# Second cross-attention of a Perceiver block: rounding the scaled values on GpSimd and VectorE in f16, and a third probability copy for VectorE in every fourth head

## The reference, cut to what matters

```python
q = _fq_sym(q, axis=-1); k = _fq_sym(k, axis=-1)
v = _fq_sym(v, axis=2)                   # s = max|v| over the tokens / 127; round(v / s) * s
attn = softmax(einsum('bhqd,bhkd->bhqk', q, k))
attn = _fq_unsigned(attn, axis=-1)       # s = max / 255; round(attn / s) * s
out = einsum('bhqk,bhkd->bhqd', attn, v)
```

## Time and profile before

| | |
|---|---|
| median of 3 runs | 692.86 us (692.32 to 695.34) |
| the profiled execution | 691.79 us, span 689.9 us from the first to the last instruction |
| the stage of the change | about 360 to 570 us of the span |
| VectorE, ScalarE, TensorE, GpSimd busy from 458 to 470 us | 11.93, 11.93, 10.00, 11.02 of 12 us |
| mean granted TensorE clock | 0.921 of full speed |

### The profile page before, as it was taken

The page is one execution under the profiler, slowest core; times in us unless marked ns, Lnnn a source line. Parts: engine busy times, 40 slices in busy tenths (PEclk is TensorE's granted clock), DMA queues, the critical chain, the costliest instruction groups (busy, mean ns, idle before and its releaser), DMA issues. The chain is left out here.

```text
span 689.9 us, 12529 instructions
## 1 busy us (share of the span) xinstructions
PE 599.5 (87%) x4685; PEld 407.8 (59%) x4685; DVE 482.6 (70%) x793; ACT 383.2 (56%) x722; POOL 330.0 (48%) x264
## 2 busy tenths in 40 slices
PE   4976899997899999988876698888988877989997
PEld 3542445444677777676752455565555565668886
DVE  4357999995565664367686899999999956433322
ACT  4227975551432222155876799999999954321110
POOL 1009999995122332033432898989899840000000
PEclk9999999997999999999995678898878889999999
DMA  8526500000936555025563888988798738900000
GB/s 345 238 74 263 228 0 1 0 1 4 298 114 209 196 175 182 11 67 152 158 183 91 166 166 155 168 137 189 135 174 156 144 63 340 385 1 1 0 1 16
DMA packets 97090, 92.89 MB, mean 135 GB/s; under 512 B 70595, under 2 KB 88323, under 8 KB 93638
## 3 DMA queue, kind: packets, MB, share of 16 engines
q1 hardware_dynamic: 84352, 85.74, 45.7%
q10 hardware_dynamic: 12678, 6.36, 3.2%
HBM read 68.59 MB, written 6.62 MB: 109 GB/s over the span
## 5 line engine op out<-in xcount | busy, mean ns | idle before, releaser
L2074 DVE TENSOR_REDUCE d_nmax<-d_psum 128x1 f32<-128x1024 f32 x128 | 152.2, 1215 | 5.8 <-PE d_psum L2230 5.8
L2230 PE MATMUL d_psum<-kst,qT 96*128 96x512 bf16 x256 | 96.6, 477 | 31.8 <-ACT d_e L2171 12.9
L528 POOL TENSOR_TENSOR b_h<-b_h,b_cb 128x1024 f32<-128x1024 f32 x32 | 88.0, 2749 | 6.5 <-DVE b_h L578 6.0
L2054 POOL TENSOR_SCALAR d_rounded<-d_e,d_lift 128x1024 f16<-128x1024 f32 x64 | 73.2, 1144 | 13.4 <-issue 7.4
L2171 ACT ACTIVATE d_e<-d_psum,d_nmax 128x1024 f32<-128x1024 f32 x64 | 71.3, 1117 | 12.7 <-DVE d_nmax L2074 12.1
L2054 POOL TENSOR_SCALAR d_rounded<-spare,d_lift 128x1024 f16<-128x1024 f32 x62 | 70.1, 1131 | 14.4 <-ACT d_lift L2175 10.2
L578 DVE TENSOR_TENSOR_SCAN b_h<-b_dA,b_psum 128x1024 f32<-128x1024 f32 x32 | 73.2, 2286 | 2.5 <-ACT b_dA L633 2.0
L2171 ACT ACTIVATE spare<-d_psum,d_nmax 128x1024 f32<-128x1024 f32 x64 | 71.3, 1118 | 1.9 <-DVE d_nmax L2074 1.9
L633 ACT ACTIVATE b_dA<-b_dtT,b_A 128x248 f32<-128x248 f32 x128 | 53.7, 490 | 33.1 <-DVE b_h L578 28.1
L2257 PEld LDWEIGHTS d_psum<-d_ident_f,d_rounded 128*128 128x128 f16 x512 | 45.4, 123 | 32.1 <-issue 21.6
L689 PE MATMUL b_psum<-b_bdiag,b_dtx 128*128 128x512 f32 x128 | 60.2, 594 | 0.8 <-DVE b_h L578 0.8
(11 more groups left out here) (430 smaller groups left out, 1168.7 us busy)
## 6 DMA issues: line engine op xcount, KB each, us to landing
c_w<-in_w0gu SPq DMA_DIRECT2D x16, 768.0 KB, 4.8
kst<-kT_scratch SPq DMA_DIRECT2D x84, 128.0 KB, 2.7
w<-in_w SPq DMA_DIRECT2D x5, 1920.0 KB, 21.3
b_cb<-c_scratch SPq DMA_DIRECT2D x4, 2048.0 KB, 7.0
c_w<-in_w0dn SPq DMA_DIRECT2D x16, 384.0 KB, 5.5
kT_scratch<-k_kT ACTq DMA_DIRECT2D x15, 384.0 KB, 2.8
a_ctx<-in_ctx SPq DMA_DIRECT2D x2, 2048.0 KB, 19.8
k_ctxT<-in_ctxT SPq DMA_DIRECT2D x12, 256.0 KB, 3.1
```

The source lines that it names most:

```text
L528: nc.gpsimd.tensor_tensor(hv, hv, cv, ALU.mult).then_inc(hc_ready, 1)
L2054: nc.gpsimd.tensor_scalar(tile_of(r, j), e[j], lift[t][:, f:f + 1], HALF_ULP_ONE, ALU.mult, ALU.add).then_inc(r_ready, 1)
L2074: nc.vector.tensor_reduce(nm[:, t, m:m + 1, f:f + 1], quarter(m, j).unsqueeze(1), AX.X, ALU.max, negate=True).then_inc(nm_ready, 1)
L2230: last = nc.tensor.matmul(quarter(m, j)[:, b * 512:(b + 1) * 512], qT[0:QROWS, m:m + 1, t * P:(t + 1) * P], kst[m % 2][0:QROWS, at:at + 51 ...
```

## The change

The values are now rounded in two steps. GpSimd takes the scaled values, multiplies by a column of ones and adds 1536 into an f16 tile (`lift_values`); VectorE subtracts 1536 from that tile. `lift_values(m)` is issued in GpSimd's pass m when j is 5, that is between the roundings of units 4 and 5, and VectorE's `round_values(m)`, still at the end of its pass, now waits for it. Besides, in passes where (m - 1) mod 4 is 3, the turned unit 7 is copied by VectorE and not by ScalarE.

```diff
+HALFWAY = 1536.0
...
-    EVEN = tuple(j for j in BY_PE if j % 2 == 0)
-    ODD = tuple(j for j in BY_PE if j % 2 == 1)
+    BY_VECTOR = ((4, 6), (4, 6), (4, 6), (4, 6, 7))
+    BY_SCALAR = tuple(tuple(j for j in BY_PE if j not in own) for own in BY_VECTOR)
...
+        vhl = [sb(f"d_vh_lifted{s}", [P, NKC, HD], F16) for s in range(2)]
+        one = sb("d_one", [P, 1])
...
                 nc.gpsimd.memset(unlift[:, :], -HALF_ULP_ONE).then_inc(ident_ready, 1)
+                nc.gpsimd.memset(one[:, :], 1.0).then_inc(one_ready, 1)
...
+                def lift_values(m, s):
+                    if m == 0:
+                        pool.wait_ge(one_ready, 1)
+                    pool.wait_ge(vhf_ready, m + 1)
+                    nc.gpsimd.tensor_scalar(vhl[s][:, :, :], vhf[s][:, :, :], one[:, 0:1], HALFWAY, ALU.mult,
+                                            ALU.add).then_inc(vhl_ready, 1)
+
                 def round_head(m, s):
                     if m >= 1:
                         scale_values(m, s)
...
                         if m == 0 and j == QT:
                             scale_values(m, s)
                         t, f = j // QT, j % QT
+                        if j == QT + 1:
+                            lift_values(m, s)
                         if m == H - 1 and j in (APH - 2, APH - 1):
                             continue
                         pool.wait_ge(lift_ready, m * TC + (t + 1))
                         pool.wait_ge(e_ready, m * APH + (j + 1))
...
                 def round_values(m):
                     s = m % 2
-                    dve.wait_ge(vhf_ready, m + 1)
+                    dve.wait_ge(vhl_ready, m + 1)
                     if 2 <= m < H:
                         dve.wait_ge(av_done, m + 1)
-                    nc.vector.tensor_scalar(vh[s][:, :, :], vhf[s][:, :, :], ROUND, ROUND, ALU.add, ALU.subtract)\
-                      .then_inc(vh_ready, 1)
+                    nc.vector.tensor_scalar(vh[s][:, :, :], vhl[s][:, :, :], -HALFWAY, None, ALU.add).then_inc(vh_ready, 1)
...
-                        if j in EVEN and 1 <= m < H + 1:
-                            copy_even(m, j)
+                        if 1 <= m < H + 1 and j in BY_VECTOR[(m - 1) % len(BY_VECTOR)]:
+                            copy_turned(m, j)
...
-                        if j in ODD and 1 <= m < H + 1:
-                            copy_odd(m, j)
+                        if 1 <= m < H + 1 and j in BY_SCALAR[(m - 1) % len(BY_SCALAR)]:
+                            copy_turned(m, j)
```

More of the change, by code:

```diff
@@ L1946, in xattn1_stage @@
         turned_in = [sem(f"d_turned_in{u}") for u in range(2)]
-        even_copied = sem("d_even_copied")
-        odd_copied = sem("d_odd_copied")
+        vector_copied = sem("d_vector_copied")
+        scalar_copied = sem("d_scalar_copied")
         av_done = sem("d_av_done")
@@ L1954, in xattn1_stage @@
         vh_ready = sem("d_vh_ready")
+        one_ready = sem("d_one_ready")
+        vhl_ready = sem("d_vhl_ready")
         o_ready = sem("d_o_ready")
@@ L1986, in head_cols, with count, wait_copied @@
             return slice(h * HD, (h + 1) * HD)
+        def count(copies, heads):
+            return sum(len(copies[h % len(copies)]) for h in range(heads))
+        def wait_copied(eng, h, j):
+            for copied, copies in ((vector_copied, BY_VECTOR), (scalar_copied, BY_SCALAR)):
+                own = copies[h % len(copies)]
+                if j in own:
+                    eng.wait_ge(copied, count(copies, h) + own.index(j) + 1)
         def tile_of(a, j):
@@ L2079, in search, with copy_turned @@
                                                 accum_out=mb[:, t, m, QT - 1:QT]).then_inc(mb_ready, 1)
-                def copy_even(m, j):
+                def copy_turned(m, j):
                     t, f = j // QT, j % QT
@@ L2086, in copy_even @@
                     nc.vector.tensor_scalar(pT[1 - m % 2][:, t, f * CPQ:(f + 1) * CPQ, :].rearrange("p c q -> p (c q)"),
-                                            turn_tile(m, j), -HALF_ULP_ONE, None, ALU.add).then_inc(even_copied, 1)
+                                            turn_tile(m, j), -HALF_ULP_ONE, None, ALU.add).then_inc(vector_copied, 1)
                 def finish(m):
@@ L2176, in exps, with copy_turned @@
                                              bias=mb[:, t, m:m + 1, QT - 1]).then_inc(lift_ready, 1)
-                def copy_odd(m, j):
+                def copy_turned(m, j):
                     t, f = j // QT, j % QT
@@ L2183, in copy_odd @@
                     nc.scalar.activation(pT[1 - m % 2][:, t, f * CPQ:(f + 1) * CPQ, :].rearrange("p c q -> p (c q)"),
-                                         turn_tile(m, j), ACT.Copy, bias=-HALF_ULP_ONE).then_inc(odd_copied, 1)
+                                         turn_tile(m, j), ACT.Copy, bias=-HALF_ULP_ONE).then_inc(scalar_copied, 1)
                 def round_last():
@@ L2242, in bank_free @@
                         if before != "values" and 1 <= back <= H:
-                            copied, some = ((even_copied, EVEN), (odd_copied, ODD))[before % 2]
-                            pe.wait_ge(copied, (back - 1) * len(some) + some.index(before) + 1)
+                            wait_copied(pe, back - 1, before)
                             return
@@ L2269, in values @@
                     else:
-                        pe.wait_ge(even_copied, m * len(EVEN) - len(EVEN))
-                        pe.wait_ge(odd_copied, m * len(ODD) - len(ODD))
+                        pe.wait_ge(vector_copied, count(BY_VECTOR, m - 1))
+                        pe.wait_ge(scalar_copied, count(BY_SCALAR, m - 1))
                     for b in range(NKC):
```

## The result

The changed kernel has a median of 741.21 us in 4 runs (737.59 to 741.96), against 693.79 us for the kernel before in its 4 runs; the ratio is 1.068, with a 95% interval of 1.064 to 1.072. The prediction was 740.4 us. The profiled execution took 740.62 us, with a span of 738.6.

What follows compares the result with a forecast made beforehand. VectorE and ScalarE were taken as tied bound. Twelve periods of 14.9 and three of 14.5 us gave +46.2, the tail +1.3: +47.5 on 691.79 makes 739.3, plus 1.07 gives 740.4 us; range 731 to 750.

Steps and rivals of the forecast that it cites:

- Part 1: VectorE's round_values waits in every head for lift_values, behind GpSimd's rounding of unit 4; period 14.9 us instead of 11.62.
- x: Time of GpSimd's new multiply-and-add over 512 elements in lift_values, taken as 0.69 us.
- Rival (c): GpSimd's new operation is as slow as the scaling, 1.26 us, 0.57 more in 16 heads: 749.5 us, chance 0.06.
- Part 2: VectorE's round_values, now one operation on f16 input, saves 0.1 us off the 0.43 of head 0.
- Rival (d): VectorE's subtraction collides with GpSimd in each head, 0.75 us more: 751.5 us, chance 0.06.
- rival (a): The wait for lift_values never ends last, so only savings of 3 us count: 689.8 us, chance 0.04.
- Part 3: Third copy moves from ScalarE to VectorE inside the wait, worth 0.4 us: 14.5 us in three of 15 periods.
- Part 4: Memset of the ones, GpSimd's own load of 11.5 us, TensorE's 10 us and the key loads cost nothing.
- the tail: After the last head's unit 4 rounding, the last finish comes 1.3 us later, at about 568.0 on the old scale.
- (b): The wait is half covered, only GpSimd's two operations, 1.9 us per head, are added: 725 us, chance 0.05.

Runs made afterwards that it cites:

- experiment 1: Changed kernel with lift_values moved to directly behind scale_values: 696.29 us against 692.65 for the kernel before, ratio 1.006.
- experiment 2: Kernel before with only scale_values moved to between GpSimd's roundings of units 4 and 5: 751.29 us, ratio 1.088.
- experiment 3: Changed kernel with a second GpSimd instruction of the same form ahead of the one in lift_values: 750.97 us, ratio 1.087 to the kernel before.
- experiment 4: Changed kernel with round_values later in VectorE's list: one search later 722.13 us, ratio 1.045; four searches later 697.53 us, ratio 1.008.
- experiment 6: Changed kernel with lift_values directly behind scale_values and no third copy: 694.86 us; also the kernel before with f32 round_values one search later: 690.46 us, ratio 0.997.

## Why the prediction was right

**Part 1, the place.** Right in mechanism and price. The 15 periods of `round_values` took 604.75 - 381.66 = 223.1 us, where 12 x 14.9 + 3 x 14.5 = 222.3 was forecast. Taking the price from head 0 of the kernel before, the one head that already had this wait, gave the chain whole, handovers included. Experiments 1 and 2 show that the place is the cause, from both sides; 3 and 4 show that the chain's length is paid one for one (0.79 us in each period for 0.78 added).

**x, the new GpSimd instruction.** 692 ns against 0.69, from the slope of two fills. The 769 ns that the Trainium skill (GPSIMD Engine Reference, Performance versus the Vector engine) gives for such a length was too high by 0.08 us here. Rival (c), 1.26, falls.

**Part 2, VectorE's saving.** 294 ns against 423 undisturbed, 0.13 less; the forecast had 0.1, the estimate from the Trainium skill (VectorE: DVE Perf Modes, Side-by-side) 0.13: the trace agrees. Rival (d), the collision, doesn't touch the subtraction in the changed kernel, since the wait itself puts it into GpSimd's gap; I had it the wrong way round. But its mechanism is real in the other kernels, up to 1175 ns, and once in the changed one, in the tail (below). In rival (a) the savings were priced at 3 us; with the place put right (experiments 1 and 6) the kernels are 3.6 and 2.7 us slower, not 3 faster. The longer subtraction can account for part of it: by the traces VectorE's 16 `round_values` took 12.0 us in experiment 1, against 9.7 in the kernel before; what GpSimd's added 0.78 us per head does was not separated. This is the one size in the text that was wrong in sign.

**Part 3, the third copy.** Three periods came out at 14.40, 14.74 and 14.39 us where 14.5 was forecast, the others at 14.9 to 15.0. In the second of them VectorE's search waited 0.26 us for TensorE.

**Part 4 and the tail.** From GpSimd's last rounding of unit 4 to the last `finish` passed 10.31 us, before 8.65: +1.7, forecast +1.3. The forecast took VectorE's own rounding of the last head's unit 6 at its old length. It now starts inside a GpSimd rounding and takes twice as long, and TensorE's turnings wait for the `finish` that stands behind it in VectorE's list. The kernel before, then the changed one (GpSimd, VectorE, TensorE):

```profile
557.95 0.75 DVE L2114 TENSOR_SCALAR d_rounded<-spare,d_lift 128x1024 f16<-128x1024 f32 x1 [1.23 <-ACT d_lift L2175]
```

```profile
604.81 1.34 POOL L2080 TENSOR_SCALAR d_rounded<-spare,d_lift 128x1024 f16<-128x1024 f32 x1
...
605.16 1.53 DVE L2139 TENSOR_SCALAR d_rounded<-spare,d_lift 128x1024 f16<-128x1024 f32 x1
...
606.93 1.86 PE L2281 MATMUL d_psum<-d_ident_f,d_rounded 128*128 128x128 f16 x16 [1.91 <-DVE d_o L2117]
```

How much of the 0.4 us that the forecast lacks is due to it was not tested. Two terms were not foreseen and cancel each other. The stage began 2.1 us earlier in this profiled execution (first rounding of unit 0 at 373.56, not 375.70); over the traces of all twelve kernels here it lies between 372.1 and 375.7, so that is not the change's. And from the last `finish` to the last addition (566.66 to 569.47 before, 613.13 to 617.92 after) passed 2.0 us more. The projection at that point, the eight matmuls in the timeline and the window around them, first of the kernel before, then of the changed one:

```profile
567.41 1.95 PE L2306 MATMUL d_psum<-d_wp,d_oT 128*128 128x256 f32 x8
...
567.00:569.50 2.50, 2.23 (x10) 1.64 (x10) 0.71 (x3) 0.70 (x2) 0.00 (x0) 1.00 0.00 0
```

```profile
614.25 3.56 PE L2330 MATMUL d_psum<-d_wp,d_oT 128*128 128x256 f32 x8 [0.21 <-ACT d_oT L2223]
...
614.00:618.00 4.00, 3.60 (x9) 2.53 (x8) 0.23 (x2) 0.47 (x2) 0.00 (x0) 0.57 0.00 0
```

Eight matmuls took 3.56 us at a mean granted clock of 0.57, mostly the lower level of 1.2 GHz, where they had taken 1.95 at 1.00. In the kernel that rounds one search later and has none of the change (experiment 6) they took 3.78, so this is not bound to the change either. They took 3.08 us or more in every trace but that of the kernel before, from which the forecast was made; that the two terms cancel to 0.1 us is luck. The sum by the traces: -2.1 + 2.0 (head 0) + 48.8 (15 periods, 223.1 against 174.3) - 2.2 (from the last `round_values` to the last `finish`, 8.38 against 10.57, for `round_values` now stands later) + 2.0 + 0.2 after it = 48.7, the difference of the spans.

**The rivals.** (a) falls with the waits. (b) falls with the period: 3.3 us were added to the 11.6 and not 1.9, so a pause does not make ScalarE so much faster afterwards.

## What to carry to other kernels

An instruction that an in-order engine waits for must be placed by what stands ahead of it in the queue of the engine that makes it, not by what it needs itself: here its input had been ready for some 9 us. Look for a head or a stage of the present kernel where the wait that a change adds already exists (a first iteration, often), and read the price of the whole loop from it. And where a result is needed two passes later, put the waiting instruction as late in the waiter's list as its user allows, before counting what its faster form saves.

## What was not expected of the hardware

One VectorE instruction on 512 f16 elements in SBUF took 284 to 1175 ns, depending on where GpSimd stood in an instruction of its own; its f32 form 416 to 1280 ns. In the traces the long cases end a fixed time behind the end of GpSimd's instruction, 0.14 to 0.15 us for the f16 form and 0.28 for the f32 one, and moving it to a quieter place brought the median down by 100 ns. The Trainium skill (GPSIMD Engine Reference, Key points) has the two engines share their SBUF interfaces, with contention for VectorE's 2-port modes; these runs agree on the contention, though no trace names the mode, and add the size: up to the rest of a GpSimd instruction, here 0.9 us.
